# A recurrent layer on one core: VectorE's scans and sums interleaved within a slot

## What is computed

```
def step(state, xs):
    d_t, B_t, C_t, u_t = xs
    dA = jnp.exp(d_t[..., None] * A)
    state = dA * state + (d_t * u_t)[..., None] * B_t[:, None, :]
    y_t = jnp.einsum('bdn,bn->bd', state, C_t)
    return (state, y_t)
```

## Time and profile before

| | |
|---|---|
| three executions, us | 1199.61, 1201.54, 1201.55 |
| the profiled execution, us | 1197.73 |
| its span from first to last instruction, us | 1195.9 |
| busy PE / DVE / POOL / ACT, us | 1068.4 / 1049.6 / 1008.5 / 710.2 |
| mean granted TensorE clock | 0.960 of full speed |
| scans L1007 on DVE | 512 of mean 1205 ns |
| sums L934 on DVE | 321 of mean 732 ns |
| dBu L770 on POOL | 256 of mean 2382 ns |
| dA L581 on ACT | 512 of mean 688 ns |

### The profile page before, as it was taken

How to read it: one execution, slowest core, us unless ns; L and a number is a source line. 1 busy time by engine, 2 the same in 40 slices (tenths; PEclk the granted TensorE clock), 3 DMA queues, 4 the chain that set the end, 5 groups by cost and what they waited for, 6 DMA issues and landing times.

```text
span 1195.9 us, 16709 instructions
## 1 busy us (share of the span) xinstructions
PE 1068.4 (89%) x5072; PEld 764.7 (64%) x5072; DVE 1049.6 (88%) x1248; ACT 710.2 (59%) x1155; POOL 1008.5 (84%) x542
## 2 busy tenths in 40 slices
PE   5979886888999979998997997998998999999767
PEld 4757665566657767675756786576756787555444
DVE  4478789899989999899987999899998999888985
ACT  4667646776574846577583665576576575464440
POOL 3589997999978898889977897879988889878961
PEclk9979998799999999999999998999999999999978
DMA  4537553443224443343322463424323443334410
GB/s 133 206 128 239 187 185 129 139 155 132 90 87 152 170 175 118 121 155 129 107 81 100 166 203 117 152 103 160 107 96 107 161 160 124 119 101 150 141 61 36
DMA packets 46566, 160.82 MB, mean 134 GB/s; under 512 B 5355, under 2 KB 5611, under 8 KB 37004
## 3 DMA queue, kind: packets, MB, share of 16 engines
q1 hardware_dynamic: 45424, 159.14, 38.9%
q10 hardware_dynamic: 1052, 0.59, 0.2%
HBM read 135.33 MB, written 24.38 MB: 134 GB/s over the span
## 4 chain that ended last, share of the span: by engine, by line
PE 47%; DVE 18%; POOL 16%; issue 14%; ACT 3%; DMA 1%; DVEq 1%; SPq 0%; POOLq 0%; ACTq 0%
PE pj L1068 15%; PE hT L1353 10%; DVE sb_h L1007 9%; POOL sb_dBu L770 8%; PE pj L1266 7%; DVE sb_yT L934 4%; PE pj L1300 4%; PE pj L1331 3%; POOL sb_yT L740 3%; PE pj L1086 2%; PE pj L1371 2%; DVE sb_un L855 2%; POOL sb_un L714 1%; POOL sb_w_sp L709 1%; PE pj L1073 1%
## 5 line engine op out<-in xcount | busy, mean ns | idle before, releaser
L770 POOL TENSOR_TENSOR sb_dBu<-sb_v,sb_bb 128x1024 f32<-128x1024 f32 x256 | 606.8, 2382 | 34.1 <-DVE sb_h L1007 26.6
L1007 DVE TENSOR_TENSOR_SCAN sb_h<-dA,sb_dBu 128x512 f32<-128x512 f32 x512 | 596.2, 1205 | 42.1 <-POOL sb_dBu L770 29.2
L581 ACT ACTIVATE dA<-sb_delta,sb_apar 128x512 f32<-128x512 f32 x512 | 345.0, 688 | 252.8 <-DVE sb_h L1007 248.6
L1068 PE MATMUL pj<-sb_x_hi,sb_w_sp 128*128 128x512 f32 x1208 | 347.6, 411 | 22.8 <-DVE sb_un L855 12.0
L1353 PE MATMUL hT<-sb_ident,sb_h 128*128 128x128 f32 x2048 | 290.0, 284 | 83.2 <-DVE sb_yT L934 68.1
L1353 PEld LDWEIGHTS hT<-sb_ident,sb_h 128*128 128x128 f32 x2048 | 244.4, 145 | 167.6 <-DVE sb_yT L934 52.9
L1068 PEld LDWEIGHTS pj<-sb_x_hi,sb_w_sp 128*128 128x128 f32 x1208 | 222.2, 194 | 85.4 <-issue 23.4
L934 DVE SCALAR_TENSOR_TENSOR sb_yT<-hT,sb_cs,sb_yT 128x512 f32<-128x512 f32 x321 | 228.4, 732 | 46.1 <-PE hT L1353 45.5
L740 POOL TENSOR_TENSOR sb_yT<-sb_yT,sb_part 128x512 f32<-128x512 f32 x155 | 198.8, 1283 | 68.0 <-ACT sb_part L674 67.8
L674 ACT ACTIVATE sb_part<-hT,sb_cs_act 128x512 f32<-128x512 f32 x155 | 106.0, 684 | 160.2 <-PE hT L1353 151.9
L1068 PE MATMUL pj<-sb_x_lo,sb_w_sp 128*128 128x512 f32 x604 | 167.6, 400 | 0.0
(11 more groups left out here) (119 smaller groups left out, 816.4 us busy)
## 6 DMA issues: line engine op xcount, KB each, us to landing
sb_w_sp<-w_cache SPq DMA_DIRECT2D x55, 1024.0 KB, 4.8
sb_ring<-w_ring SPq DMA_DIRECT2D x67, 512.0 KB, 3.4
sb_bb<-b_rows SPq DMA_DIRECT2D x128, 256.0 KB, 3.7
w_cache<-sb_w_sp SPq DMA_DIRECT2D x19, 1024.0 KB, 4.8
sb_xio<-x SPq DMA_DIRECT2D x7, 1024.0 KB, 7.2
out<-sb_xio SPq DMA_DIRECT2D x3, 1024.0 KB, 5.7
sb_xio<-x SPq DMA_DIRECT2D x4, 256.0 KB, 3.7
out<-sb_xio SPq DMA_DIRECT2D x4, 256.0 KB, 2.0
```

The costliest lines, as they stand in the source:

```text
L581: nc.scalar.activation(dA[g % 2][:, :], delta[:, j, :], ACT.Exp, scale=apar[:, j, n:n + 1]).then_inc(dA_done, 1)
L770: nc.gpsimd.tensor_tensor(dBu[:, dbu_buffer(s), :, :], v[:, j:j + 2, :], bb[:, i % B_RING, :].unsqueeze(1).to_broadcast([P, 2, T]), ALU.mu ...
L1007: nc.vector.tensor_tensor_scan(h[:, i % 2, 2 * part + e, :], dA[g % 2][:, :], dBu[:, dbu_buffer(s), e, :], 0.0, ALU.mult, ALU.add).then_in ...
L1068: done = nc.tensor.matmul(bank[:, :], w[:, kk * P:(kk + 1) * P], xs[:, kk, :], start=(p == 0), stop=(p == len(products) - 1))
```

## The change

VectorE's order within a slot: scan, sum of a tile, scan, sum of the other tile, in place of both scans and then both sums. Nothing is added or removed; no wait, buffer or semaphore changes.

```
                     nc.vector.tensor_tensor_scan(h[:, i % 2, 2 * part + e, :], dA[g % 2][:, :], dBu[:, dbu_buffer(s), e, :],
                                                  0.0, ALU.mult, ALU.add).then_inc(scan_done, 1)
-                    for c in (2 * part, 2 * part + 1):
+                        c = g % TC
                         if i > 0 and (i - 1, c) in ON:
                             add_state(b, i - 1, c)
                         elif i == 0 and not first and (UNITS - 1, c) in ON:
```

## The result

The changed kernel took 1214.15 us (median of 4, 1211.78 to 1217.24); the kernel before, run beside it, 1201.55 (median of 4, 1199.61 to 1204.55). The medians lie 12.6 us apart. The ratio of the runs, which is not that of the medians, is 1.0112, 95% interval 1.0078 to 1.0145, or 13.5 us more, with 9.4 to 17.4 as bounds. The forecast was 15.7 us more, 1217.

What follows compares the result with a forecast made beforehand. No single bound: VectorE and TensorE take turns waiting for each other. Terms 9.9 + 3.4 + 2.4 = 15.7 us on 1197.73 give 1213.4, or 1217 against the median 1201.54; range 1206 to 1224.

Steps and rivals of the forecast that it cites:

- VectorE's own work costs nothing in either order: In every slot: scans at 1.13 us and sums at 0.66 keep their spacing, so VectorE's own work costs the same.
- no-change rival: Whole kernel: same operations and every wait absorbed, so 1201.5 us; chance 0.08.
- Place A: Slot (5, 1) of each batch: ScalarE's second dA waits for the later second scan; 1.8 + 3 * 2.7 = 9.9 us.
- predicted signs: Slot (5, 1), batch 1: about 2.0 us before first sum, ScalarE idle some 2.5, slot (6, 1) dA wait above 1.0.
- Place B: End of batches 0 to 2, slot (29, 1): ScalarE's next activation 1.14 us later, 1.1 an end, 3.4 us.
- Place C: Slot (10, 1) of batches 2 (0.9) and 1 (0.3), slot (25, 1) of batches 0 to 2 (0.4 each): 2.4 us.
- Most of the 27 us is paid back: 33 slots with a late first tile: lateness of about 27 us, mostly regained while VectorE waits in the following even slot.
- Batches 4 to 5 us longer, batch 3 under 3: Profile after: batches grow by 4 to 5 us, batch 3 by under 3.
- the clock's bound: TensorE's clock falling at seven new pauses of 1.5 us each: 10.5 us more if none is covered.
- Slower by more through the clock at the new pauses: About 1228 us: TensorE's clock falls at new pauses, or little of the 27 us is paid back; chance 0.11.
- Faster through the bank freed early: Even slots of units 30 and 31: first tile's bank freed 1.13 us earlier, 9 us gained, 1192.5; chance 0.06.
- Slower by less: About 1207 us: ScalarE catches up in slot (5, 1), leaving 5.8 us from the other places; chance 0.13.

Runs made afterwards that it cites:

- e6: Interleaved order in eleven slots of each batch whose first tile is early or nearly so, against the kernel before: 1200.76 against 1198.45 us, ratio 1.0008.
- e3: Changed order everywhere, with ScalarE's second dA of slot (6, 0) in its own buffer, against the kernel before: 1204.97 us, ratio 1.0055.
- e4: Kernel before, with ScalarE's second dA of slot (6, 0) also waiting for both sums of slot (5, 1), against the kernel before: 1204.49 us, ratio 1.0041.
- e1: Interleaved order in slot (5, 1) of each batch alone, against the kernel before: 1208.21 against 1199.58 us, ratio 1.0080.
- e12: Interleaved order in slot (10, 1) alone, against the kernel before: 1199.88 against 1200.37 us, ratio 0.9999.
- e2: The change in all its slots except (5, 1), against the kernel before: 1206.89 us, ratio 1.0057.
- e5: Interleaved order in slots (29, 1) and (30, 0) alone, against the kernel before: 1205.47 us, ratio 1.0057.
- e11: Interleaved order in slot (30, 0) alone, against the kernel before: 1200.46 us, ratio 0.9998.
- e8: Order of before, with ScalarE's second dA of slot (6, 0) in its own buffer, against the kernel before: 1200.25 against 1198.45 us, ratio 1.0013.
- e7: Interleaved order in slots (1, 1), (2, 1), (3, 1) and (4, 1) alone, against the kernel before: 1201.42 against 1198.45 us, ratio 1.0025.
- e10: Interleaved order in slot (29, 1) alone, against the kernel before: 1204.31 against 1200.37 us, ratio 1.0034.
- e9: The kernel before once more, same instructions on every engine, against the kernel before: 1199.70 against 1200.37 us, ratio 0.9997.

## Why the prediction was right, and where it was off

*VectorE's own work costs nothing in either order:* right. Busy 1049.7 against 1049.6, and e6 shows no cost clear of the noise in 43 slots. The Trainium skill, "VectorE: DVE Perf Modes", section "The DRAIN you can't avoid", says that the same eight operations took the same time with a semaphore after each as with one after the last. The trace agrees in so far as VectorE's busy time didn't change. The no-change rival that was made of it fell, because the cost is on ScalarE.

*Place A, 9.9 us:* right in mechanism and size. The trace has 9.98, and each batch its predicted value to 0.04. Timed alone it is 9.6 (7.6 to 11.6). e3 takes ScalarE's wait away and leaves 0.69, e4 adds the wait to the old order and gets 8.2, both in the trace. The predicted signs were there: 1.97 before the first sum (2.0 expected), ScalarE idle 2.68 (2.5), VectorE's wait for dA grown from 1.02 to 2.64. The shift reaches the end of the batch nearly whole: in batch 1 the row from (6, 1) to (29, 1) is 0.00 after and -0.17 in e1.

*Place B, 3.4 us:* right. 3.24 in the trace, 4.1 (2.3 to 5.9) timed for slot (29, 1) alone, and nothing for slot (30, 0), covered as the prediction said.

*Place C, 2.4 us:* mis-sized, 1.3 in the trace after, and of another nature than I took it for. Slot (10, 1) of batch 2 cost 1.33 in the trace after, where I had 0.9, and nothing in e12. In batch 1, where I had 0.3, the stretch around it cost nothing after, 1.5 in e2 and e3 and 0.43 in e12, but also 0.45 in e5, which has no edit there. I read one execution's tile times as fixed. Slots (25, 1), 3 times 0.4, cost nothing, and this step failed for a reason to see. VectorE did come 0.5 late to slot (26, 0) in batches 0 to 2, and by slot (26, 1) it had all of it back. VectorE's and GpSimd's timeline of batch 1 in slot (26, 0), after the change:

```profile
594.28 1.99 DVE L870 TENSOR_SCALAR sb_ms<-sb_ms 128x4 f32<-128x4 f32 x1
...
594.97 1.27 POOL L740 TENSOR_TENSOR sb_yT<-sb_yT,sb_part 128x512 f32<-128x512 f32 x1
```

Before, that L870 began at 587.01 and took 2.50; it began 7.27 later and ended 6.76 later. The 0.5 that VectorE had lost before it came back inside an instruction whose end goes with GpSimd's. In batches 0 to 2 it took 1.99 to 2.10 us in the three kernels in which slot (25, 1) is interleaved (after, e2, e3), and 2.47 to 2.59 in the eleven others. A list of idle times doesn't show such cover.

*"Most of the 27 us is paid back":* right as far as can be told. The stretches of the trace put down to the change are A 9.98, B 3.24, slot (10, 1) 1.33, and the slots ahead of A in batches 1 to 3 (0.43, -0.76, 0.47) 0.14: 14.7 us, against 15.7 forecast and 13.5 (9.4 to 17.4) measured. The rest of the 19.5 is the 2.16 and 1.70 of the table's rows that go with the clock and 1.0 ahead of A in batch 0, of which e11 has as much without an edit there. That the 2.16 isn't the change's is argued from e8's 2.32, not shown: an edited slot lies in it. VectorE's waits for transposes grew by 11 us, not by some 20. e7 leaves a doubt, 3.0 us (1.2 to 4.8) for four slots that I had at nothing.

*Batches 4 to 5 us longer, batch 3 under 3:* off for three of the four. From first scan to first scan batches 0 to 2 grew by 3.34, 4.25 and 6.67 us, batch 3 to its slot (31, 1) by 5.0. For batch 0 the prediction's own terms give 3.3 (1.8, 1.1 and 0.4), and not 4 to 5. The excess is in the stretches that vary from one execution to the next: 2.16 at slot (1, 1) of batch 2 and the clock's 1.70 in batch 3.

*The range.* Its high end, 1224, was said to be the sum with a third of the clock's bound. A third of 10.5 us gives 1220.7; 1224 takes two thirds.

*The rivals.* Slower by more through the clock at the new pauses: present at one of the two told of here, and it cost nothing there. At A TensorE's new pause came out at 1.28 and the clock stayed at 1.00 behind it. At B the pause at the end of batch 1 is 2.54 (1.65 before), and in the window behind it the clock fell to 0.52, about 1.2 GHz, where before it was 1.00:

```profile
633.00:636.00 3.00, 3.00 (x11) 2.54 (x10) 3.00 (x4) 2.61 (x5) 3.00 (x3) 0.52 0.00 0
```

No more than B's 1.08 was lost at that end, since VectorE then waits 2.09 for GpSimd anyway. Faster through the bank freed early: e11 frees it 1.1 us early in batch 3, and the wait for the second sum takes it all, as the prediction said against this rival. Slower by less: A was there in full.

## What to carry to other kernels

An instruction moved behind a wait on an in-order queue delays everyone who waits for it, and the price is set by what stands in the waiter's queue: here VectorE's earlier wait was free in most slots and cost 2.7 us in the one where ScalarE had a second dA and behind it two table loads and six activations queued on the scan, and 1.1 at the end of three batches. So before an operation that may wait is moved ahead of one that doesn't, list who is released by the second, and look for the places where that engine has no idle time. No version tried beats the order of before; both scans first is the safer order where a tile can be late.

## What was not expected of the hardware

**The clock's fall after the same pause.** TensorE's timeline in batch 3, at the last tile of unit 11, before and in e10, whose nearest edit is over 120 us away:

```profile
1017.46 0.66 PE L1353 MATMUL hT<-sb_ident,sb_h 128*128 128x128 f32 x4 [1.94 <-DVE sb_yT L934]
1018.10 3.67 PE L1266 MATMUL pj<-sb_u,sb_ring 128*128 128x512 f32 x8
```

```profile
1022.99 0.66 PE L1361 MATMUL hT<-sb_ident,sb_h 128*128 128x128 f32 x4 [1.95 <-DVE sb_yT L936]
1023.63 5.37 PE L1274 MATMUL pj<-sb_u,sb_ring 128*128 128x512 f32 x8
```

A pause of 1.94 was followed by eight products in 3.67 us, one of 1.95 by the same eight in 5.37, with a granted clock of 0.57 over 4 us. Two profiles of the same kernel (before and e9) agree to 0.24 us in every stretch of the table, but the short stretch was slow in 8 of 14 profiles and the long one fast in 5, in no relation to the edits that I can find. Both profiles of the order before are among those with neither, so it can't be excluded that any edit, wherever it is, makes them likelier. These two and slot (1, 1) of batch 2 move a profile by up to 3.3 us each, which is of the size of the spread of the runs (1198.37 to 1205.30 in e7). What tips them is open.

**A 128x4 operation of 2 us.** The L870 above ended at 596.27, and GpSimd's L740 at 596.24. Before, they ended at 589.51 and 589.49. In batches 0 and 2 of before it is the same (312.53 and 312.51, 871.64 and 871.61), so the operation seems to be held until GpSimd pauses, through the end of one of its operations and the whole of the next. In all 14 profiles and all three batches it starts inside GpSimd's dBu and ends 0.03 after GpSimd's next operation. Ahead of batch 0, where GpSimd is idle, it took 0.17 in every profile. In before:

```profile
50.00 0.17 DVE L870 TENSOR_SCALAR sb_ms<-sb_ms 128x4 f32<-128x4 f32 x1
```

The Trainium skill, "SBUF — State Buffer", section "Who interferes with whom", says that VectorE in a two-port mode and GpSimd share a pair of ports, and that whoever issues first keeps it for the whole instruction. The trace fits this, with the addition that the hold lasted over two GpSimd instructions. Which mode the operation runs in no run shows, and no run took GpSimd's work away, so that the ports are the cause is inferred from the ends and from the 0.17.
